# Transposing the first two tiles of y by DMA instead of on TensorE, with VectorE scaling them in place

## The reference

```python
x = x + tanh(g_xattn) * matmul(fake_quant(layernorm(x)), fake_quant(ctx))      # per batch, 2 x (1024 x 2048 x 2048)
y = layernorm(x)
x = x + tanh(g_ffn) * (y @ W_up^T + delta)                                     # 2048 x 2048 x 2048
# delta: top-1 of 4 experts by y @ gate_w^T + bias; z = y @ lora_A[e]^T (rank 8); delta = z @ lora_B[e]^T
```

## Time and profile before

| | us |
|---|---|
| median of 3 runs | 959.64 |
| lowest and highest | 959.42, 960.67 |
| the profiled execution, own time | 959.95 |
| its span, first to last instruction | 958.1 |
| TensorE busy | 936.5 |
| VectorE busy | 472.3 |
| ScalarE busy | 234.5 |
| POOL busy | 17.1 |

### The profile page before, as it was taken

The page is one execution under the profiler, slowest core; times in us unless marked ns, Lnnn a source line. Parts: engine busy times, 40 slices in busy tenths (PEclk is TensorE's granted clock), DMA queues, the critical chain, the costliest instruction groups (busy, mean ns, idle before and its releaser), DMA issues.

```text
span 958.1 us, 12470 instructions
## 1 busy us (share of the span) xinstructions
PE 936.5 (98%) x5253; PEld 501.1 (52%) x5278; DVE 472.3 (49%) x1022; ACT 234.5 (24%) x196; POOL 17.1 (2%) x40
## 2 busy tenths in 40 slices
PE   3999999999999999999999999999999999999998
PEld 2444444444455555555555555555555555555554
DVE  7774757785884715343342615343342615343321
ACT  6975776777650100000000000000000000000000
POOL 0001100000000000000000000000000000000000
PEclk9999999999999999999999999999999999999999
DMA  8999987688652332222223233222223222121211
GB/s 350 422 405 406 377 318 271 227 302 290 221 152 88 111 110 44 88 44 89 44 89 88 66 111 45 88 44 88 45 88 88 61 72 44 45 45 44 44 44 44
DMA packets 77081, 135.26 MB, mean 141 GB/s; under 512 B 61936, under 2 KB 62080, under 8 KB 62720
## 3 DMA queue, kind: packets, MB, share of 16 engines
q1 hardware_dynamic: 71088, 92.74, 30.1%
q0 software_dynamic: 3488, 24.92, 6.7%
q10 hardware_dynamic: 2448, 16.78, 4.3%
HBM read 90.38 MB, written 29.37 MB: 125 GB/s over the span
## 4 chain that ended last, share of the span: by engine, by line
PE 96%; ACT 2%; DVE 1%; DMA 1%; issue 0%; SPq 0%; ACTq 0%
PE bank L1085 71%; PE bank L1003 22%; PE bank L1094 1%; PE bank L980 1%; ACT arena L414 1%; DMA rows<-in_x 1%; DVE bn L598 0%; ACT rows_T L402 0%; ACT halves L384 0%; PE bank L1077 0%; DVE arena L669 0%; SPq L282 0%; PE bank L1100 0%; DVE ln L602 0%; ACT ln L378 0%
## 5 line engine op out<-in xcount | busy, mean ns | idle before, releaser
L1085 PE MATMUL bank<-arena,rows_T 128*128 128x416 f16 (+1 forms) x3840 | 683.4, 339 | 0.0
L1085 PEld LDWEIGHTS bank<-arena,rows_T 128*128 128x128 f16 x3840 | 372.4, 97 | 304.3
L1003 PE MATMUL bank<-arena,rows_T 128*128 128x512 bf16 x999 | 222.8, 381 | 3.7 <-DVE arena L669 2.5
L1003 PEld LDWEIGHTS bank<-arena,rows_T 128*128 128x128 bf16 x1024 | 99.5, 98 | 120.6 <-issue 4.8
L783 DVE SCALAR_TENSOR_TENSOR rows<-bank,derived,rows 128x416 f32<-128x416 f32 (+2 forms) x80 | 49.8, 640 | 213.9 <-PE bank L1085 213.9
L453 ACT ACTIVATE z_stack_T<-bank 96x128 f16<-96x128 f16 x16 | 4.4, 273 | 560.1 <-PE bank L1100 560.1
L598 DVE BATCH_NORM_STATS2 bn<-rows 128x6 f32<-128x512 f32 x124 | 76.7, 678 | 5.9 <-DMA rows<-in_x 5.7
L723 DVE SCALAR_TENSOR_TENSOR route<-bank,derived,scal 128x4 f32<-128x4 f32 x16 | 3.5, 221 | 113.2 <-PE bank L1085 113.2
L659 DVE SCALAR_TENSOR_TENSOR rows<-bank,derived,rows 128x512 f32<-128x512 f32 x60 | 44.7, 748 | 25.0 <-PE bank L1003 24.6
L791 DVE SCALAR_TENSOR_TENSOR rows<-bank,z_back_scale,rows 128x512 f32<-128x512 f32 x64 | 45.1, 746 | 10.6 <-PE bank L1094 6.6
L699 DVE SCALAR_TENSOR_TENSOR halves<-normed,ln,halves 128x2048 f16<-128x2048 f32 x14 | 32.9, 2351 | 29.0 <-ACT halves L447 29.0
(11 more groups left out here) (106 smaller groups left out, 293.0 us busy)
## 6 DMA issues: line engine op xcount, KB each, us to landing
arena<-in_ctx SPq DMA_DIRECT2D x22, 1024.0 KB, 16.4
stage<-in_w SPq DMA_DIRECT2D x17, 1042.0 KB, 5.5
out<-rows ACTq DMA_DIRECT2D x15, 1024.0 KB, 3.9
h_scratch<-rows POOLq DMA_DIRECT2D x11, 1024.0 KB, 9.5
rows<-h_scratch SPq DMA_DIRECT2D x11, 1024.0 KB, 4.9
stage<-in_ctx SPq DMA_DIRECT2D x10, 1024.0 KB, 9.9
rows<-in_x POOLq DMA_DIRECT2D x10, 1024.0 KB, 9.2
normed<-in_w SPq DMA_DIRECT2D x7, 1042.0 KB, 6.5
```

The costliest lines, as they stand in the source:

```text
L1003: mm = mmul(bk, q1T[:, t % 4, kt, :], Q(b, n, kt), start=(kt == 0), stop=(kt == KT - 1 and not slow), skip_group_check=True)
L1085: mm = mmul(bank[c][:, 0:b - a], YT[:, s % 2, yh, kt, :], W(kt, wh, a, b), start=(first and kt == kts[0] and yh == 0 and wh == 0), stop=(k ...
```

## The change

The 64 transposes on TensorE and VectorE's `yT_out` go. Each of the first two tiles of y is transposed by the same kind of DMA as the others, and `yT_scale(s, g)` multiplies the group of four k in YT in place (SBUF to SBUF). SP issues `y_transpose(0)` between loads 17 and 18 of W, and `y_transpose(1)` behind the load of the back-scale row. `y_high(s)` now waits for the DMA transpose of the tile before. On VectorE `moments(16)` moves from period 14 to the last slot of period 13, ahead of `epi(13, 3)`; `norm(0)` to slot a and `y_low(0)` to slot b of period 14. On ScalarE the square root of tile 16 moves ahead of `abs_sum(13)`, and `y_high(0)` ahead of `abs_sum(15)`. The four groups of tile 0 are scaled between `w_low(9)` and `b_scale()`, two of them between the last three `epi`.

```diff
@@ -34,7 +34,7 @@
     HEAD = 4
     LEAD = 3
     KEEP = 4
-    BY_PE = 2
+    UNSCALED = 2
     HALF = KT // 2
 
     BY_V = [(1, 0), (2, 1), (3, 1)]
@@ -165,8 +165,6 @@
 
         bank = [es.enter_context(nc.psum_tensor(f"bank{i}", [P, NB], F32)) for i in range(8)]
         TR = [bank[5][:, :], bank[6][:, :]]
-
-        YB = [[TR[0], TR[1], bank[7][:, :], TR[0]], [TR[0], TR[1], TR[0], TR[1]]]
         ZP = bank[7][:, :].bitcast(F16)[0:ZR, 0:P]
 
         s_scal = sem("scal_loaded"); s_braw = sem("b_loaded"); s_bs = sem("b_abs_sum"); s_bp = sem("b_pow")
@@ -190,7 +188,7 @@
         s_sum = sem("w_abs_sum"); s_wp = sem("w_pow"); s_wa = sem("w_scale"); s_hi = sem("w_high")
         s_lo = sem("w_ready")
         s_pm = sem("pow_max"); s_PM = sem("pow_max_all")
-        s_yh = sem("y_high"); s_yl = sem("y_low"); s_yt = sem("yT_group"); s_ye = sem("yT_out")
+        s_yh = sem("y_high"); s_yl = sem("y_low"); s_ye = sem("yT_scaled")
         s_wc = sem("w_back_scale"); s_wr0 = sem("w_back_row_parked"); s_wr = sem("w_back_row_loaded")
         s_dt = sem("y_transposed_by_dma")
         s_m2 = sem("chunk2_done"); s_dl = sem("delta_done"); s_rt = sem("route_step"); s_zs = sem("z_stack_ready"); s_gl = sem("z_back_scale_ready")
@@ -300,7 +298,19 @@
             row(5)
             for c in range(16, CT):
                 ctx_tile(c)
-            for i in range(KT + 8):
+            def y_transpose(s):
+                sp.wait_ge(s_yl, s + 1)
+                if s < UNSCALED:
+                    sp.wait_ge(s_mm, place[(13 if s == 0 else 15, NCH - 1)] + 1)
+                else:
+                    sp.wait_ge(s_m2, 5 * (s - 1))
+                sp.dma_start_transpose(YT[:, s % 2].rearrange("p h k m -> p (h k) m"),
+                                       HL[:, :, :].rearrange("p h d -> p (h d)")).then_inc(s_dt, 16)
+
+            for i in range(KT + 2):
+                load_w(i)
+            y_transpose(0)
+            for i in range(KT + 2, KT + 8):
                 load_w(i)
             sp.wait_ge(s_wc, 1)
             sp.dma_start(wrow_d.rearrange("k p -> p k"), wc[:, :],
@@ -308,13 +318,11 @@
             sp.wait_ge(s_wr0, 16)
             sp.wait_ge(s_lo, KT)
             sp.dma_start(WR, wrow_d.rearrange("k p -> (k p)").unsqueeze(0).to_broadcast([P, D])).then_inc(s_wr, 16)
-            for s in range(BY_PE, TILES):
+            y_transpose(1)
+            for s in range(UNSCALED, TILES):
                 if s + 3 < TILES:
                     row(TILES + s + 3)
-                sp.wait_ge(s_yl, s + 1)
-                sp.wait_ge(s_m2, 5 * (s - 1))
-                sp.dma_start_transpose(YT[:, s % 2].rearrange("p h k m -> p (h k) m"),
-                                       HL[:, :, :].rearrange("p h d -> p (h d)")).then_inc(s_dt, 16)
+                y_transpose(s)
 
         @block.gpsimd
         def _(pool):
@@ -435,13 +443,10 @@
                 act.wait_ge(s_norm, s + 1)
                 if s == 0:
                     act.wait_ge(s_tr, 2 * TILES)
-                elif s <= BY_PE:
-                    act.wait_ge(s_yt, 4 * s)
-                    act.wait_ge(s_yl, s)
                 else:
-                    act.wait_ge(s_dt, 16 * (s - BY_PE))
+                    act.wait_ge(s_dt, 16 * s)
                 u = TILES + s
-                if s < BY_PE:
+                if s < UNSCALED:
                     A(HL[:, 0, :], Xt(u), ACT.Identity, bias=L(u, "nmr"), scale=L(u, "rstd")).then_inc(s_yh, 1)
                 else:
                     A(HL[:, 0, :], T[:, 0:D], ACT.Identity, scale=L(u, "rstd")).then_inc(s_yh, 1)
@@ -525,8 +530,8 @@
                 n = 2 * p - 17
                 period(p, lambda: (w_high(n), abs_sum(n + 1)), lambda: w_high(n + 1), lambda: abs_sum(n + 2))
             period(12, lambda: (w_high(7), abs_sum(8)), lambda: abs_sum(9), lambda: abs_sum(10))
-            period(13, lambda: abs_sum(11), lambda: abs_sum(12), lambda: abs_sum(13))
-            period(14, lambda: abs_sum(14), lambda: (sqrt(TILES), abs_sum(15)), lambda: y_high(0))
+            period(13, lambda: abs_sum(11), lambda: abs_sum(12), lambda: (sqrt(TILES), abs_sum(13)))
+            period(14, lambda: abs_sum(14), lambda: y_high(0), lambda: abs_sum(15))
             act.wait_ge(s_braw, 16)
             act.wait_ge(s_mm, place[(TILES - 2, NCH - 1)] + 1)
             A(q1T[0:ZR, (TILES - 2) % 4].rearrange("p k m -> p (k m)"), Braw, ACT.Abs,
@@ -691,22 +696,17 @@
 
             def y_low(s):
                 dve.wait_ge(s_yh, s + 1)
-                if s < BY_PE:
-                    if s >= 1:
-                        dve.wait_ge(s_yt, 4 * s)
+                if s < UNSCALED:
                     v.tensor_tensor(HL[:, 1, :], T[:, 0:D], HL[:, 0, :], ALU.subtract).then_inc(s_yl, 1)
                 else:
                     v.scalar_tensor_tensor(out=HL[:, 1, :], in0=T[:, 0:D], scalar=L(TILES + s, "rstd"), in1=HL[:, 0, :],
                                            op0=ALU.mult, op1=ALU.subtract).then_inc(s_yl, 1)
 
-            def yT_out(s, g):
-                dve.wait_ge(s_yt, 4 * s + g + 1)
-                if s < 2:
-                    dve.wait_ge(s_mm, place[(13 if s == 0 else 15, NCH - 1)] + 1)
-                src = YB[s][g].bitcast(F16).rearrange("p (h a m) -> p h a m", h=2, a=4)
-                dst = YT[:, s % 2, :, 4 * g:4 * g + 4, :]
+            def yT_scale(s, g):
+                dve.wait_ge(s_dt, 16 * (s + 1))
+                part = YT[:, s % 2, :, 4 * g:4 * g + 4, :]
                 back = wc[:, 4 * g:4 * g + 4].unsqueeze(1).unsqueeze(3).to_broadcast([P, 2, 4, P])
-                v.tensor_tensor(dst, src, back, ALU.mult).then_inc(s_ye, 1)
+                v.tensor_tensor(part, part, back, ALU.mult).then_inc(s_ye, 1)
 
             def route(s):
                 base = LINKS * s
@@ -886,17 +886,16 @@
                 n = 2 * p - 17
                 period(p, lambda: w_low(n - 1) if n > 1 else None, lambda: (w_low(n), w_pow(n + 1)), lambda: w_pow(n + 2))
             period(12, lambda: w_low(6), lambda: w_low(7), nothing)
-            period(13, nothing, nothing, nothing)
+            period(13, nothing, nothing, lambda: moments(TILES))
 
             def scales():
                 powers(HALF, KT)
                 dve.wait_ge(s_wa, KT)
                 v.tensor_reduce(V["pm"], wp[:, :], AX.X, ALU.max).then_inc(s_pm, 1)
 
-            period(14, lambda: moments(TILES), lambda: norm(0), scales)
+            period(14, lambda: norm(0), lambda: y_low(0), scales)
             epi(14, 3)
             moments(TILES + 1)
-            y_low(0)
             epi(15, 0)
             dve.wait_ge(s_PM, 1)
             step(v.reciprocal(V["rPM"], V["PM"]))
@@ -906,15 +905,15 @@
             step(v.tensor_tensor(V["gs"], V["sc2"], V["tf"], ALU.mult))
             w_low(8)
             epi(15, 1)
-            yT_out(0, 0)
-            yT_out(0, 1)
             w_low(9)
+            yT_scale(0, 0)
             epi(15, 2)
+            yT_scale(0, 1)
             epi(15, 3)
             w_low(10)
             w_low(11)
-            yT_out(0, 2)
-            yT_out(0, 3)
+            yT_scale(0, 2)
+            yT_scale(0, 3)
             b_scale()
             w_low(12)
             w_low(13)
@@ -924,12 +923,12 @@
             y_low(1)
             b_low()
             route(0)
-            yT_out(1, 0)
-            yT_out(1, 1)
+            yT_scale(1, 0)
+            yT_scale(1, 1)
             for c in range(5):
                 epi2(0, c)
-            yT_out(1, 2)
-            yT_out(1, 3)
+            yT_scale(1, 2)
+            yT_scale(1, 3)
 
             for s in range(1, TILES):
                 if s == 1:
@@ -1056,27 +1055,6 @@
                         chunk(t, n, slow)
                         if n == 0 and t + 1 < TILES:
                             transposes(t + 1)
-                        if n == 1 and t == TILES - 1:
-                            y_transposes(0, 0)
-                            y_transposes(0, 1)
-                            y_transposes(0, 2)
-                        if n == 2 and t == TILES - 1:
-                            y_transposes(0, 3)
-
-            def y_transposes(s, g):
-                if g == 0:
-                    pe.wait_ge(s_yl, s + 1)
-                if s == 0 and g < 2:
-                    half_out(TILES - 1, g)
-                elif s == 0 and g == 2:
-                    pe.wait_ge(s_epi, NCH * (TILES - 1))
-                else:
-                    pe.wait_ge(s_ye, {0: 1, 1: 4 + g - 1}[s])
-                for i in range(8):
-                    h, k = i // 4, 4 * g + i % 4
-                    mm = nc.tensor.transpose(YB[s][g].bitcast(F16)[:, i * P:(i + 1) * P],
-                                             HL[:, h, k * P:(k + 1) * P], idh[:, :])
-                mm.then_inc(s_yt, 1)
 
             def products(s, c, kts, first):
                 a, b = CUT[c], CUT[c + 1]
@@ -1091,6 +1069,8 @@
             def lora(s, j):
                 if s > 0 or j >= 2:
```

(11 more changed lines are left out.)

## The result

| | before | changed |
|---|---|---|
| median, us | 960.11 (8 runs) | 969.13 (8 runs) |
| lowest and highest | 959.42, 960.67 | 962.59, 975.17 |
| profiled execution, span | 958.1 | 963.9 (its own time 965.75) |

The changed kernel is slower: ratio 1.0098, 95% interval 1.0064 to 1.0132. The forecast was no measurable change, 960.1 in a range of 957.9 to 963.3. Two things stand out: the median moved by 9 us, and the spread from 1.3 us to 12.6 us. The profiled execution is one of the better ones, 3.4 us under the median, so its trace shows the smaller part of the loss.

What follows compares the result with a forecast made beforehand. The prediction took TensorE, busy for 98% of the span, to bound the kernel. Its terms, -3.73 + 2.5 + 1.0 + 0.7 = +0.5 us, gave a median of 960.1 us, range 957.9 to 963.3.

Steps and rivals of the forecast that it cites:

- The removed work: TensorE's chain: 64 transposes of y's tiles 0 and 1 go, -3.73 us.
- the wait of ScalarE at the square root: Stage 1, tile 16's statistics: ScalarE stands from 234.2 to 236.9 us; TensorE doesn't feel it.
- VectorE's wait for y_high(0): End of stage 1: VectorE stands from 241.0 to 244.8 us, making w_low(8) 2.2 us late.
- The gap at stage 2's start: TensorE's first product of stage 2 waits for yT_scale(0,0) until 261.5 instead of 259.04: +2.5 us.
- the second wait: First K step of stage 2: TensorE reaches chunk 3 at 263.1, its bank is free at 264.1: +1.0 us.
- The clock: TensorE's granted clock may fall behind the first gap of stage 2: 0 to +1.5 us, taken as +0.7.
- The sum: All terms against the profiled execution: -3.73 + 2.5 + 1.0 + 0.7 = +0.5 us, on the median 960.1.
- Tile 1: Stage 2's second tile: y_transpose(1), issued at 291.4, lands near 300; cost 0, upper end +1.6 us.
- The deadline of 302.0: Latest landing of y_transpose(1) without cost: two scales and epi2(0,0), 2.95 us, precede TensorE's tile 1 start at 304.9.
- A: VectorE's scales at stage 2's start run at half duration: -1.4 us, 958.2; chance 0.16, of which 0.13 over the bound.
- B: End of stage 1: VectorE waits for POOL's maximum over partitions (PM), at most 7.4 us: 963.3; chance 0.2.
- C: Ahead of tile 1: y_transpose(1) lands after 302.0, behind the row load: up to +1.6 us, 961.7; chance 0.14.

Runs made afterwards that it cites:

- e8: e3 with VectorE doing yT_scale(0, 0), epi(15, 2) and epi(15, 3) ahead of w_low(9), the other three scales later; 956.43 us, ratio 0.9959.
- e5: The changed kernel with tile 1 of y transposed by TensorE again, only tile 0 by DMA; 961.14 us, ratio 1.0009.
- e1: The changed kernel with y_transpose(1) moved ahead of the load of the back-scale row on SP's queue; 959.60 us, ratio 0.9994.
- e2: The changed kernel with POOL's load of a row tile made to wait for the landing of y_transpose(1); 959.86 us, ratio 1.0000.
- e7: The changed kernel again, unedited, on another chip; 973.5 us, ratio 1.0113.
- e3: The changed kernel with both edits: y_transpose(1) ahead of the back-scale row load, POOL's load behind its landing; 960.20 us, ratio 0.9997.
- p4: The kernel before with 0.5 MB loads added at DMA transposes of tiles 2 to 14: SP's ahead, POOL's one memset later; 962.15 us, one execution.

## Why the prediction was wrong

**What held.** The removed work is -3.73: e8 wins 3.9. The evacuations and the wait of ScalarE at the square root didn't touch TensorE. VectorE's wait for y_high(0) came, 3.64 us against 3.8. The gap at stage 2's start was 1.96 us (2.6 in e5) against 2.5, the second wait some 0.7 against 1.0. The clock cost 0 or 0.8 us net from execution to execution (1.5 less the 0.7 of the second wait, which passes under it), against 0 to 1.5, of which 0.7 was taken. y_transpose(0) landed in time. The sum's own value for the hand-over was +3.5 +0.7 -1.95 = +2.25. From the transposes near 42 us to the transpose of z the traces give, against the kernel before without its 0.89 of transposes in between, +1.1 to +1.2 with the clock kept (e1, e2, e7) and +1.9 with it low (the changed kernel and e3); e5, which has just this part, is +0.85 in the median and +1.4 in its trace. So the hand-over was put some 0.4 us too high by the traces and 1.4 by e5's median, which is small beside the miss.

**What failed** is the step "Tile 1": "It lands at 298.1 if alone, at 303.6 if the row load ahead of it delays it in full; I take 300." It landed at 306.4 in the profiled execution and at 310.5 in e7's. Its cost, "0, upper end 303.6 - 302.0 = +1.6", was 4.7 us of standing and 1.6 of clock in the first of them, and 8.9 and 2.3 in the second. The deadline of 302.0 was right (301.6 in the trace: 306.38 - 4.74), in part by luck: its tile 1 start of 304.9 leaves out the 0.7 us of clock that the sum takes, and the traced execution was 0.64 us ahead from stage 1 on. The landing was not. The upper end was worked out from the transpose's own queue alone. POOL's load from DRAM was not in it at all: it is released by b_low, at 288.98 in the kernel before and at 291.84 in the changed one, and it is on no path, for nothing depends on its landing for a long time. The change puts a transfer that TensorE waits for between two that are not urgent. e1 puts it ahead of the one, e2 holds the other back until it has landed, and the loss is gone both times.

**The rivals.** A (scales at half duration): no, 1.22 us. VectorE's rows show 1.21 us each out of PSUM in the kernel before and 1.22 out of SBUF. The double speed that the Trainium skill gives for 16-bit operands in SBUF (VectorE: DVE Perf Modes, the perf-mode tier table) didn't show here, where the second operand is the f32 back-scale. The working gave A a chance of 0.13 of passing 0.2% although its own figure, 958.2, lies within it. B (PM late): no, it came within 4.0 us, and it decides from 5.0 on. C (the transpose of tile 1 lands late) had the right place and a chance of 0.14, and its sign, TensorE standing ahead of tile 1, came; it was priced at +1.6. Its price was bounded by queue order (theory II), which e2 refutes. The range stopped at B and left the real case outside.

**What the profile before could have told.** L316's landings are 6.7 to 8.5 us with almost nothing beside them; a row of an undisturbed transfer is no upper end for one that shares the DMA engines. The Trainium skill says (DMA: Bandwidth & Descriptors, "Issuing engines are not separate DMA queues") that DMAs issued by SP and by POOL run on the same 16 DMA engines and interleave. The traces agree: POOL's load was slowed with the transpose, 12.4 and 15.7 us instead of 6.7. The skill gives no time for such a case, and no row of the kernel before has one.

## What to carry to other kernels

Before moving work from an engine to a DMA that something waits for, list every transfer of every queue that will be in flight beside it, also those that nobody waits for, and give each an upper end measured beside such neighbours. Two cheap mends are to issue the urgent transfer first and to let the others wait for its landing; either was enough here. Where an added step is to be hidden at a hand-over, put it in the order of the engine ahead of work with slack: moving one w_low and one scale behind the steps that TensorE waits for, and a further scale later, was worth 0.38% (e8 against e3).

## What was not expected of the hardware

- A DMA transpose of 1 MB lands in 6.7 us alone. With a load ahead of it on its own queue and a load of another queue issued 1.0 to 2.7 us behind it, it took 12.9 us in the median of p4 and up to 19.7 (e7), and in e7 all DMA engines together moved under 65 GB/s for 4.6 us in between, most of it idle. What holds them up is not settled: no run looks below the queues, and the longest executions, 972 to 982 us, of which there is no trace, are put down to the same landing only because e1, e2 and e3 have none of them.
- SP itself is held by the transpose it issues: 4.85 us alone, 14.37 us in the changed kernel.
- The granted clock fell behind a gap of 2.0 us in two profiled executions (the changed kernel's and e3's) and not in four others with gaps of 2.0 to 2.6. A gap of this size is thus no forecast of the clock in either direction.
